# Linear attention tile loop: the root of the mean square moves from ScalarE to GpSimd as a power, the outputs are scaled and gated at the head of VectorE's list, and even and odd heads alternate on TensorE

## What is computed

```python
q1, k1, v = (x @ Wq) * scale, x @ Wk, x @ Wv
q2 = (x @ Wqa @ Wqb) * scale
k2 = softmax((x @ Wka @ Wkb) per head)
gk1, gk2 = (log_sigmoid(x @ Wg{1,2}a @ Wg{1,2}b + bg{1,2}) / 16)
# per chunk of 64 tokens: g = cumsum(gk); A = tril((q*exp(g)) @ (k*exp(-g)).T)
# o = A @ v + (q*exp(g)) @ S;  S = S * exp(g_last) + k_out.T @ v
o = o_dense(q1, k1, v, gk1) + sum over experts of o_sparse(q2, k2, v, gk2)
o = o * rsqrt(mean(o * o, axis=-1) + 1e-5) * norm_w
o = o * (g * sigmoid(g))          # g = x @ Wga @ Wgb
return o @ Wo                     # gated and added to the residual
```

## Time and profile before

| | us |
|---|---|
| median of 3 runs (lowest, highest) | 5782.2 (5778.06, 5784.22) |
| profiled execution, its own time | 5784.91 |
| its span | 5783.2 |
| TensorE busy in the span | 4961.7 (86%) |
| VectorE busy | 4323.1 (75%) |
| ScalarE busy | 3136.3 (54%) |
| GpSimd busy | 938.3 (16%) |
| linear attention, first projections to end | about 4706 to 5783.2 |

### The profile page before, as it was taken

How to read it: one execution, slowest core, us unless ns; L and a number is a source line. 1 busy time by engine, 2 the same in 40 slices (tenths; PEclk the granted TensorE clock), 3 DMA queues, 4 the chain that set the end, 5 groups by cost and what they waited for, 6 DMA issues and landing times. The chain is left out here.

```text
span 5783.2 us, 106990 instructions
## 1 busy us (share of the span) xinstructions
PE 4961.7 (86%) x37182; PEld 2607.9 (45%) x37184; DVE 4323.1 (75%) x5246; ACT 3136.3 (54%) x5403; POOL 938.3 (16%) x886
## 2 busy tenths in 40 slices
PE   6589999999999999999932758467999879999998
PEld 3233333333333333333322336235666647677676
DVE  4589999999999999999466223466665557777777
ACT  1068888888888888888921212112222234444443
POOL 0000000000000000000007720443220013334333
PEclk8689999999999999999965879778999969999998
DMA  5322333323322222222111047421110120100000
GB/s 180 109 93 91 100 100 97 98 88 98 103 91 81 77 82 81 82 80 78 32 43 66 14 128 235 147 76 58 54 37 1 59 73 22 26 23 22 26 23 14
DMA packets 241629, 431.82 MB, mean 75 GB/s; under 512 B 37945, under 2 KB 142410, under 8 KB 239008
## 3 DMA queue, kind: packets, MB, share of 16 engines
q1 hardware_dynamic: 197424, 355.18, 19.9%
q0 software_dynamic: 26928, 62.99, 3.4%
q10 hardware_dynamic: 16896, 8.39, 0.6%
HBM read 329.36 MB, written 133.89 MB: 80 GB/s over the span
## 5 line engine op out<-in xcount | busy, mean ns | idle before, releaser
L579 DVE TENSOR_REDUCE attn_mpart<-attn_ps_max 128x2 f32<-128x1024 f32 x2048 | 2498.6, 1225 | 122.6 <-PE attn_ps_max L617 111.1
L524 ACT ACTIVATE attn_probs<-attn_ps_exp 128x512 f32<-128x512 f32 x4096 | 2222.0, 595 | 350.8 <-PE attn_ps_exp L633 103.5
L617 PE MATMUL attn_ps_max<-attn_keys,attn_quer 54*128 54x512 f32 x4096 | 1503.5, 462 | 82.2 <-DMA attn_keys<-k_laid 55.1
L633 PE MATMUL attn_ps_exp<-attn_quer,attn_keys 54*128 54x512 f32 x4096 | 1505.9, 450 | 23.6 <-issue 13.5
L648 PE MATMUL attn_ps_out<-attn_probs,attn_vals 128*32 128x256 f32 x16384 | 1317.7, 393 | 8.4 <-ACT attn_o_sb L530 7.8
L633 PEld LDWEIGHTS attn_ps_exp<-attn_quer,attn_keys 54*128 54x128 f32 x4096 | 615.1, 186 | 877.1 <-ACT attn_probs L524 839.6
L648 PEld LDWEIGHTS attn_ps_out<-attn_probs,attn_vals 128*32 128x32 f32 x16384 | 324.0, 108 | 755.8 <-issue 400.5
L617 PEld LDWEIGHTS attn_ps_max<-attn_keys,attn_quer 54*128 54x128 f32 x4096 | 602.6, 190 | 123.4 <-DVE attn_mpart L579 63.5
L1442 PE MATMUL ra_psO<-ra_vals,ra_probT 128*128 128x256 f32 x1152 | 299.7, 410 | 80.2 <-DVE ra_probT L1614 80.0
L1371 POOL DMA_INDIRECT ra_rows<-y_rows,slots x256 | 253.8, 991 | 379.6 <-DVE ra_total L1536 308.2
L1500 ACT ACTIVATE ra_row<-ra_psS 128x512 f32<-128x512 f32 x112 | 66.9, 597 | 448.7 <-PE ra_psS L1423 448.7
(11 more groups left out here) (324 smaller groups left out, 6001.5 us busy)
## 6 DMA issues: line engine op xcount, KB each, us to landing
attn_keys<-k_laid SPq DMA_DIRECT2D x256, 304.0 KB
attn_vals<-v_aug SPq DMA_DIRECT2D x128, 512.0 KB, 15.0
attn_keys<-k_laid SPq DMA_DIRECT2D x256, 128.0 KB
x_rows<-attn_zeros POOLq DMA_DIRECT2D x16, 1280.0 KB, 9.9
exp_x<-x_rows SPq DMA_DIRECT2D x64, 320.0 KB
exp_w1w<-in_w SPq DMA_DIRECT2D x64, 256.0 KB
y_rows<-exp_y SPq DMA_DIRECT2D x64, 256.0 KB
q_laid<-proj_parts SPq DMA_DIRECT2D x32, 256.0 KB
```

The source lines that it names most:

```text
L524: act.activation(probs[k % 2][:, j, :], ps_exp[bank_of(g, n)][:, :], ACT.Exp).then_inc(exp_done, 1)
L579: dve.tensor_reduce(mpart[i][:, kb, TC * pair + tile::TC * NPR], ps_max[u % 2][:, :, :], AX, ALU.max).then_inc(unit_read, 1)
L617: mm = pe.matmul(ps_max[u % 2][:, h, :], quer[g][half(h), pair, tile * P:(tile + 1) * P], keys[g % 2][half(h), pair, kb * CH:(kb + 1) * CH ...
L633: pe.matmul(ps_exp[bank_of(g, n)][:, :], keys[g % 2][half(h), pair, k * P:(k + 1) * P], quer[g][half(h), pair, :], start=True, stop=True). ...
```

## The change

The two ScalarE instructions of `rms` become one GpSimd power with exponent -0.5, first in GpSimd's list of an iteration. VectorE's `gated` is split: `scale_o` (the product with the root, read from PSUM) follows `mean_square` directly, and `gated` (the product with the gate) comes after `add_bias` and before `center`. ScalarE's `decays` moves ahead of the Ln of `log_sigmoids`. TensorE alternates even and odd heads, matmul by matmul, in `scores` and in `keys_values`; the dense scores go before `decay_sums`, the sparse ones after, and the sparse ones now wait for both dense masks.

```diff
+                pool.memset(power[:, :], -0.5).then_inc(halves_step, 1)
-                pool.wait_ge(halves_step, 1)
+                pool.wait_ge(halves_step, 2)
...
+                def root(tile):
+                    m, _, i = tile
+                    hold(pool, ms_ready, m + 1, pool_passed)
+                    pool.tensor_tensor(ms[:, :], ms[:, :], power[:, :], ALU.pow).then_inc(rms_ready, 1)
+
                 def iteration(nxt, cur, prv):
+                    if prv is not None:
+                        root(prv)
                     queries(cur)
...
-                def log_sigmoids(tile):
+                def log_sigmoids(tile, cur):
...
                     act.activation(lz[:, :, :], lz[:, :, :], ACT.Exp, scale=-1.0).then_inc(lz_step, 1)
+                    if cur is not None:
+                        decays(cur)
                     act.wait_ge(lz_step, 3 * m + 2)
                     act.activation(lz[:, :, :], lz[:, :, :], ACT.Ln, bias=1.0).then_inc(lz_step, 1)
...
-                def rms(tile):
-                    m, _, i = tile
-                    act.wait_ge(ms_ready, m + 1)
-                    act.activation(ms[:, :], ms[:, :], ACT.Ln).then_inc(rms_step, 1)
-                    act.wait_ge(rms_step, m + 1)
-                    act.activation(ms[:, :], ms[:, :], ACT.Exp, scale=-0.5).then_inc(rms_ready, 1)
...
                     if prv is not None:
                         mean_square(prv)
+                        scale_o(prv)
                     if nxt is not None:
                         add_bias(nxt)
+                    if prv is not None:
+                        gated(prv)
                     if nxt is not None:
                         center(nxt)
                     mask_scores(cur)
-                    if prv is not None:
-                        gated(prv)
...
-                def scores(tile):
-                    m, _, i = tile
-                    pe.wait_ge(feats_copied, 4 * m + 4)
-                    for x in range(4):
-                        if x >= 2:
-                            pe.wait_ge(scores_masked, 4 * m + x - 1)
-
-                        r = x % 2 * DK
-                        for b in range(NPAIR):
-                            mm = pe.matmul(psW[(x + 1) % 2][:, b * P:(b + 1) * P], ftT[r:r + DK, x // 2 * 2, b, :],
-                                           ftT[r:r + DK, x // 2 * 2 + 1, b, :], start=True, stop=True)
-                        mm.then_inc(scores_summed, 1)
+                def scores(tile, kind):
+
+                    m, _, i = tile
+                    if kind:
+                        pe.wait_ge(scores_masked, 4 * m + 2)
+                    else:
+                        pe.wait_ge(feats_copied, 4 * m + 4)
+                    for b in range(NPAIR):
+                        for odd in range(2):
+                            r = odd * DK
+                            mm = pe.matmul(psW[1 - odd][:, b * P:(b + 1) * P], ftT[r:r + DK, 2 * kind, b, :],
+                                           ftT[r:r + DK, 2 * kind + 1, b, :], start=True, stop=True)
+                            if b == NPAIR - 1:
+                                mm.then_inc(scores_summed, 1)
...
-                    for hh in range(HL):
-                        head, rows = slice(hh * DK, (hh + 1) * DK), slice(hh % 2 * DK, hh % 2 * DK + DK)
-                        for e in range(NE):
-                            pe.matmul(psS2[rows, hh // 2, e, :], ke[i][:, e, head], v[i][:, head], start=True, stop=True)
-                        mm = pe.matmul(kv1[rows, hh // 2, :], kg1[i][:, head], v[i][:, head], start=True, stop=True)
+                    for b in range(NPAIR):
+                        for e in range(NE + 1):
+                            for odd in range(2):
+                                head, rows = slice((2 * b + odd) * DK, (2 * b + odd + 1) * DK), slice(odd * DK, odd * DK + DK)
+                                dst, keys = (kv1[rows, b, :], kg1[i][:, head]) if e == NE else (psS2[rows, b, e, :], ke[i][:, e, head])
+                                mm = pe.matmul(dst, keys, v[i][:, head], start=True, stop=True)
...
                     ahead(ZG, K2)
+                    scores(cur, 0)
                     decay_sums(cur)
-                    scores(cur)
+                    scores(cur, 1)
                     ahead(Q2, V)
```

More of the change, by code:

```diff
@@ L1905, in linear_attention @@
         sq, on = sb("sq", [P, HL, DK]), sb("on", [P, HL, DK])
-        ms = sb("ms", [P, HL])
+        ms, power = sb("ms", [P, HL]), sb("power", [P, HL])
         oT = sb("oT", [P, NPAIR, P])
@@ L1923, in linear_attention @@
          ke_ready, qe_ready, feats_turned, feats_copied, scores_summed, scores_masked, a_ready, dec_summed,
-         dec_exped, kv_summed, kv_read, state_set, state_done, intra_inter, squared, ms_ready, rms_step, rms_ready, o_step, o_read,
+         dec_exped, kv_summed, kv_read, state_set, state_done, intra_inter, squared, ms_ready, rms_ready, o_step, o_read,
          on_ready, o_turned, o_copied, y_summed, y_read, y_step, y_ready) = (
@@ L1929, in linear_attention @@
                 "ke_ready qe_ready feats_turned feats_copied scores_summed scores_masked a_ready "
-                "dec_summed dec_exped kv_summed kv_read state_set state_done intra_inter squared ms_ready rms_step rms_ready "
+                "dec_summed dec_exped kv_summed kv_read state_set state_done intra_inter squared ms_ready rms_ready "
                 "o_step o_read on_ready o_turned o_copied y_summed y_read y_step y_ready").split())
@@ L1994, in _ @@
                                    pattern=[[0, 1]], channel_multiplier=1).then_inc(halves_step, 1)
-                pool.wait_ge(halves_step, 3)
+                pool.wait_ge(halves_step, 4)
                 pool.tensor_scalar(rwq[:, :], erw[:, :], QSCALE, None, ALU.mult).then_inc(const_set, 1)
@@ L2041, in iteration @@
                         keys(nxt)
-                run(pool, prologue, iteration, lambda tile: None)
+                run(pool, prologue, iteration, root)
             @block.scalar
@@ L2113, in iteration @@
                     if nxt is not None:
-                        log_sigmoids(nxt)
-                    if prv is not None:
-                        rms(prv)
-                    decays(cur)
+                        log_sigmoids(nxt, cur)
+                    else:
+                        decays(cur)
                     if nxt is not None:
@@ L2126, in prologue @@
                 def prologue(tile):
-                    log_sigmoids(tile)
+                    log_sigmoids(tile, None)
                     q2_and_v(tile)
@@ L2131, in epilogue @@
                 def epilogue(tile):
-                    rms(tile)
                     copy_o(tile)
@@ L2154, in add_bias, with scale_o @@
                         dve.tensor_tensor(zb[:, x, :], psP[:, x, :], bias[:, x, :], ALU.add).then_inc(biased, 1)
-                def gated(tile):
+                def scale_o(tile):
                     m, _, i = tile
@@ L2162, in gated @@
                                       ALU.mult).then_inc(o_read, 1)
+                def gated(tile):
+                    m, _, i = tile
                     dve.wait_ge(o_read, m + 1)
@@ L2292, in epilogue @@
                     mean_square(tile)
+                    scale_o(tile)
                     gated(tile)
```

## The result

The changed kernel takes 5800.1 us (median of 7 runs), the kernel before 5778.06 us in the runs beside it: a ratio of 1.0047, interval 1.0036 to 1.0059. By the medians that is 22 us slower, by the ratio 27, where 37 us faster was forecast; 5800 lies outside the range, whose end was 5785.

A forecast was written before the change was run, and what follows sets the result against it. Three tiles of four were bound by TensorE's own work at a falling clock, one by the root's detour. A tile 1.13 us shorter over 31 tiles (35 us) plus 1.6 at the end gave 37 us less: 5745 us, range 5688 to 5785.

The forecast's parts named there:

- The forecast tile: Linear attention loop: mean of three tiles with a clock fall (32.9) and one without (29.9), 32.15 us against 33.28.
- The power and the scaling ahead of the bias: Head of VectorE's list: power taken at 0.3 us plus 0.2 for semaphores; ZG waits 0.65, K2 starts about 1.1 later.
- I take 0.3 (nearest in engine and size): GpSimd's root power: length taken near the 8-element half masks (0.21 us), as no power is in the trace.
- The bound above it, 1.7: GpSimd's root power: upper bound on its length, about 1.7 us, from the ScalarE detour that it replaces.
- rival 3: Head of VectorE's list: a slow power delays biases, masks and TensorE; at 1.7 us 5788, at 2 us 5797; chance 0.12.
- I see no clear direction and keep three in four: TensorE's clock in the loop: still falls in three tiles of four, each fall costing 3.0 us.
- Rival 4: TensorE's clock stays down longer because TensorE stands before ZG and the sparse scores: 5817, or 5769 at today's length; chance 0.11.
- The pairs: TensorE's keys_values: alternating heads let column halves work side by side, 3.56 to some 2.4 us; gain 1.15, bounds 0 and 1.2.
- A full-clock tile of 29.9: Loop tile without a clock fall: 32.3 - 1.7 (wait) - 1.15 (pairs) + 0.5 (Q2, late masks) = 29.9 us.
- The price of a fall, 3.0: TensorE's clock: a tile with a fall takes 33.6 us, one without fall or wait 30.6, so a fall costs 3.0.
- The wait on L2350: TensorE before turning the outputs: its 1.69 us wait, in one tile of four, was to go.
- The wait for the dense masks: TensorE before the sparse scores: a new wait of about 1 us, eating the gain of the dense pairs.

The follow-up runs named there:

- e13: The changed kernel with 16 unused TensorE passes filling its wait between the transposes and ZG; ratio to the kernel before 1.0017, loop 1039.7 us.
- e1: The changed kernel with GpSimd multiplying by the constant instead of raising to the power, so the root is left out; ratio to the kernel before 0.9926.
- e5: The changed kernel with scores and keys_values as before and decay passes ahead of all scores; ratio to the kernel before 1.0326.
- e12: The changed kernel with TensorE's old list and a GpSimd product instead of the power, root left out; ratio to the kernel before 1.0195.
- e2: The changed kernel with VectorE's scaling and gating moved back behind the four masks; ratio to the kernel before 0.9836, loop 944.6 us.
- e3: The kernel before with one edit, keys_values matmuls alternating between even and odd heads; ratio 0.9967, loop 1008.0 us.
- e4: The kernel before with the root as a GpSimd power and ScalarE's decays ahead of Ln, VectorE's and TensorE's orders kept; ratio 0.9996.
- e10: The changed kernel with scaling and gating between dense and sparse masks, plus eight unused passes ahead of the decay passes; ratio to the kernel before 0.9790.
- e9: The changed kernel with eight unused full-row passes on TensorE directly ahead of the decay passes; ratio to the kernel before 1.0124.

## Why the prediction was wrong

**The sum with the measured terms.** The forecast tile was 32.15 us. The power took 1.65, not 0.3: +1.35. The clock fell in four tiles of four, not three: +0.25 x 3.2 = 0.8, with 3.2 the difference of the steady tile (34.1) and the one tile without a fall (30.9, e13). Together 34.3; measured 34.1. Over 31 tiles the two terms are +42 and +25 us, and -35 + 42 + 25 = +32, against +29.5 measured over the loop. The close fit is in part luck: the first eleven tiles had longer falls than the sum counts, and the short last tile was faster.

**The step that failed** is the part "The power and the scaling ahead of the bias", in the sentence "I take 0.3 (nearest in engine and size)". The half masks are of the same engine and size, but a product and no power; the length of a power could not be read from them. It is 1.65 us. e1 puts a product of 0.2 us in its place and measures 5743, next to the forecast of 5745. The bound above it, 1.7, held, and rival 3 said what it would cost (at 1.7 a time of 5788). The range ended at 5785, so it left out the time of the sum's own bound. That rival deserved far more than 0.12: no row spoke for the lower value.

**The second failure** is the sentence "I see no clear direction and keep three in four". The clock fell in every tile, for 7.5 us in the mean where the sum had 5.1. Rival 4 had this, but apart from rival 3. e1 shows that the two come together: with the short product at the same place the mean is 5.3 us. In the old order of TensorE the same head costs more still (e5, 17 us in a tile, 186 us in all). That TensorE's standing is the link, as rival 4 has it, is not shown: e12 has a long fall with a wait of 0.6 us, and e13 keeps the fall in the steady tile with the wait filled.

**What held.** The mechanism of the power's price (rival 3) is confirmed by e1, e2, e5 and e12. The pairs: 80 passes of keys_values take 2.64 us in the changed kernel's chain and 1.1 us leave the full-clock tile in e3, for 1.15 forecast; the rule of the Trainium skill (TensorE: Matmul & The Clock Gate, Part 3), by which only row groups overlap their weight loads, would leave no gain for these column halves, and the measured 1.1 us speak against it, as rows 7 had. A full-clock tile of 29.9 was forecast with a power of 0.3; e1, with 0.21, has 29.6. But its path through a tile was not all as forecast: the four tiles of e1 are two with 10.2 us at the low clock and two with none, not three with 6.8 and one with none. That the means agree (5.3 and 5.1 us) is luck. The price of a fall, 3.0, was 3.2. The wait on L2350 went. The gating takes 1.63 beside GpSimd (1.74 forecast). The sum's step of 0.11 us for the first four score passes is misread ((0.71 - 0.27) / 3 = 0.15), but nothing hangs on it: sixteen alternating passes take 1.06 to 1.28 us in e2 and the changed kernel, for 1.2 expected. The wait for the dense masks, forecast at 1 us, is only 0.18 us (L2370 above): its cause, late masks, was there, but TensorE came late as well, by the wait ahead of ZG. At the end of the kernel VectorE waits 1.86 us, not 0.5.

**What stayed open.** The runs do not show why the falls of TensorE's clock distribute over tiles as they do, and give no rule by which four of four could have been foretold. They do show that the order of VectorE's list alone moves them (e4 against e5 and e12), and that filling TensorE's wait at the head does not (e13, steady tile).

## What to carry to other kernels

An operation that moves to another engine must be priced by that same operation there; where the trace has none, put its whole range into the forecast, and put it where its length is hidden: VectorE waits for the same eight-element power once in the loop of e2, and in every tile of the changed kernel, where it costs 60 us against a short product. Even a short operation can stand badly at the head of a list that TensorE waits for: e1 is 52 us over e2, e12 117 over e4, most of that, by my estimate, by the clock. One reordering of VectorE's list (e2) got 113 us back. Judge a part of a change alone and in the company it will have: the pairs were worth 20 us in the old order, with a third to a half of the work saved given back by the clock.

## What the runs showed of the hardware that was not expected

- GpSimd's power of 128 x 8 elements takes 1.65 us (1.646 to 1.680 over 32), a product of the same size 0.20 to 0.21.
- VectorE's log-sigmoid step on three operands of 1536 elements takes 3.35 us on average in the changed kernel, 1.75 before. Before, `add_scores` had ended when it started; now they overlap for 2.0 us in the tile shown (VectorE's row, then GpSimd's):

```profile
L2192 DVE SCALAR_TENSOR_TENSOR gla_ls<-gla_zb,gla_lz 128x1536 f32<-128x1536 f32 x30 | 100.5, 3350 | 16.5 <-ACT gla_lz L2076 16.5
...
5535.44 3.62 DVE L2192 SCALAR_TENSOR_TENSOR gla_ls<-gla_zb,gla_lz 128x1536 f32<-128x1536 f32 x1 [0.52 <-ACT gla_lz L2076]
...
5535.09 2.35 POOL L2022 TENSOR_TENSOR gla_a<-gla_a 128x1024 f32<-128x1024 f32 x1 [2.81 <-DVE gla_a L2186]
```

- VectorE's product of 128 x 512 with the gate takes 0.69 us with GpSimd idle, 1.63 to 1.74 and, in e4, 2.44 us beside GpSimd's work.
- The clock's low stretches per tile were 0, 3, 7, 10, 13.5 and 17 us in these kernels, at nearly the same work. In e3, with less work, their mean rose from 5.6 to 7.1 us; with unused work added they went in e10 and became irregular in e9.
- The changed kernel's steady tile is 34.1 us with and without 1.95 us of filler in its wait.
